# A fused cross-attention and feed-forward kernel on one core: the order of the set-up work in its opening and of a few steps between its two stages is changed

## The chip, the core and the metric

The kernel runs on one core of a Trainium2 chip. The metric is the device time of one execution in microseconds, as the median of three executions; lower is better. A core has five engines that run their own instruction streams and meet at semaphores: TensorE (PE in the profile), VectorE (DVE), ScalarE (ACT), GpSimd (POOL) and SyncE (SP), which here only issues DMAs. ScalarE issues three DMAs too.

## The reference

Sixty-four sequences of 64 tokens with 128 features each attend to a context of the same shape, then pass a feed-forward layer. The set-up draws biases and gammas that are not zero and one, so nothing can be left out.

```
def _L0_xattn_ref(x, c, Wq, bq, Wkv, bkv, q_gamma, k_gamma):
    q = x @ Wq.T + bq                       # x is the layer norm of the input
    kv = c @ Wkv.T + bkv                    # 16 heads of 8, k and v interleaved
    q = _rms_norm(q, q_gamma); k = _rms_norm(k, k_gamma)
    scores = jnp.einsum('bhnd,bhmd->bhnm', q, k) * scale
    attn = jax.nn.softmax(scores, axis=-1)
    out = jnp.einsum('bhnm,bhmd->bhnd', attn, v)
def _L0_ffn_ref(x, w1, b1, w2, b2):
    h = float2fix(jnp.einsum('bsd,df->bsf', x, w1) + b1, 8)
    h = float2fix(pwlin_gelu_basic(h, 8, 8), 8)   # linear between 33 points of an exact GELU
    return float2fix(jnp.einsum('bsf,fd->bsd', h, w2) + b2, 8)
x = x + _L0_xattn_ref(_layernorm(x), ctx_1024, ...)
x = x + _L0_ffn_ref(_layernorm(x), ...)
```

## The kernel before

The 4096 tokens are 32 tiles of 128. The attention takes two tiles a step, in 16 steps (0 to 15); the feed-forward layer takes four tiles a group, in 8 groups of two units each. Everything is written out by hand: each engine has its own program, in which `step(s)` issues that engine's share of several steps at once (a software pipeline), and every wait is on a semaphore. So each engine works strictly in the order of its code.

**A step of the attention.** GpSimd normalises x (`norm_x`, L309 to L315). TensorE transposes context and x into `bank_in` (`transpose_in`, L943 and L948), ScalarE copies that to `xcT` (L430), TensorE projects to q, q with gammas and k (`project_qk`, L955 to L964) and v (`project_v`, L974). ScalarE squares (L435), VectorE sums the squares per head (`mean_square`, L617), ScalarE takes logarithm and exponential (L441, L444), VectorE normalises (L624) and writes 16-bit high parts (L635); GpSimd writes the low parts (`lows`, L334). TensorE transposes the parts (`transpose_parts`, L992, eight matmuls for each of two tiles), ScalarE and VectorE copy them out (L450, L644), TensorE makes scores (L1006), ScalarE exponentials (L460), TensorE multiplies by v (`times_v`, L1022) and transposes back (`out_back`, L1032), and VectorE divides (`heads_out`, L664 and L666). GpSimd adds the residual (L341); VectorE takes the statistics of the second layer norm (`ln2_statistics`, L606) and applies it (`norm_x2`, L611, two instructions a step).

**Biases.** A bias enters as a matmul of a 16-bit selector (`pick16`) with `b_parts`, in which each bias row is split into three 16-bit parts. `bias_parts` makes them on VectorE in five dependent stages: cast (L719), subtract (L721), cast (L723), subtract (L725), cast (L727). This is done once for the attention's biases (384 columns) and once for those of the feed-forward layer (640 columns). Before, the bias matmul opens each accumulation (`start=True`) and the data matmuls follow.

**The opening.** SyncE loads x 0, context 0, the two gammas and `bkv` (these three broadcast to all partitions and counted by one semaphore, `small_loaded`, together with ScalarE's load of `b_q`), then x 1 to x 3 and context 1, each x waiting for the one before it, then the four loads of the feed-forward layer. VectorE clears two of the four `v_blk` buffers (L590), GpSimd the other two (L382), after its share of step -1. VectorE copies the transposed weights (L698 to L704), waits for `small_loaded`, and makes `gqk` (L732), the bias rows, `bound_sq` (L744), `wqgT` (L749) and the attention's bias parts. `bound_sq` is read by every engine (`guarded`, L226): a large value takes a branch with a slower, safe pass over all tiles; with these inputs it is not taken. No engine gets past this place before `bound_sq` is there.

**The feed-forward stage.** TensorE: `hidden` (L1128 for the bias, L1129) and `down` (L935, L1144). ScalarE rounds (L513) and evaluates the GELU at two points, `gelu_low` (L521) and `gelu_high` (L530). VectorE splits the rounded value into `f_segment` (L829) and `f_fraction` (L835), and makes `f_rise` (L842), `f_slope` (L850), `f_round` (L856) and `f_out` (L862). GpSimd adds (`f_interpolate`, L406); it waits for the slope of its own unit and the fraction of the next but one:

```
wait(pool, "slope_done", n + 1)
if gr + 1 < GROUPS:
    wait(pool, "frac_ready", n + UNITS + 1)
```

## Time and profile before

| what | value |
|---|---|
| median of three executions | 220.64 us (218.24 to 221.98) |
| profiled execution, device time | 219.01 us |
| profiled execution, span from first to last instruction | 217.1 us |
| mean granted TensorE clock | 0.959 |
| TensorE, matmuls | busy 184.1 us, 85% of the span |
| VectorE | busy 189.3 us, 87% |
| ScalarE | busy 146.3 us, 67% |
| GpSimd | busy 117.9 us, 54% |

The span starts with the first instruction, and all times in the rows count from there; 1.9 us of the profiled execution's time lie outside it. A busy share is a mean over stages with different limits, so where time can be won has to be read from the timeline. A matmul's end is modelled and overlaps the next one's start.

### The profile page before, as it was taken

Reading aid. Unit: us, or ns where it says so; the run is one execution under the profiler, and the core shown is the slowest. Engines: PE = TensorE matmul, PEld = TensorE weight load, DVE = VectorE, ACT = ScalarE, POOL = GpSimd, SP = SyncE. Lnnn points to the kernel's source line nnn. Section 1 sums busy time; section 2 is a strip of 40 time slices with the busy share of each in tenths; the row PEclk is TensorE's granted clock in tenths of the full one; section 3 lists DMA queues with packets and bytes.
Section 4 is the critical chain, followed back from the end, with each engine's and each line's share of the span. In section 5 each row is a group of like instructions: output and inputs, shape, how many; then the busy total and the mean of one; then the engine's idle time right before and its main releaser. Section 6 shows DMA issues by size and latency. Waiting matters only on the chain.

```text
span 217.1 us, 8020 instructions
## 1 busy us (share of the span) xinstructions
PE 184.1 (85%) x3308; PEld 143.5 (66%) x3308; DVE 189.3 (87%) x348; ACT 146.3 (67%) x226; POOL 117.9 (54%) x166
## 2 busy tenths in 40 slices
PE   1172889999999999999999789959799999986693
PEld 0161768888888888888888645456566566654592
DVE  6628968799999999999999757999999999999992
ACT  2021367778977778987777778867487878878511
POOL 7330864687677687767675501465165444655430
PEclk9996699999999999999999999988999999999679
DMA  4270111011211011100000000000101011010103
GB/s 110 82 206 10 51 53 49 14 44 51 54 53 49 27 32 53 51 27 29 8 3 3 3 3 2 3 0 0 48 5 48 0 48 51 0 48 0 48 0 97
DMA packets 14835, 7.95 MB, mean 37 GB/s; under 512 B 1072, under 2 KB 14576, under 8 KB 14800
## 3 DMA queue, kind: packets, MB, share of 16 engines
q1 hardware_dynamic: 14272, 7.20, 11.6%
q8 instruction: 26, 0.43, 0.8%
q10 hardware_dynamic: 528, 0.25, 0.4%
q14 instruction: 9, 0.07, 0.1%
HBM read 5.35 MB, written 2.10 MB: 34 GB/s over the span
## 4 chain that ended last, share of the span: by engine, by line
PE 44%; DVE 23%; issue 13%; POOL 13%; DMA 2%; ACT 1%; SPq 1%; DVEq 0%; POOLq 0%; ACTq 0%
POOL y_raw L406 8%; PE bank_o L1022 8%; PE banks_p L992 7%; PE banks_p L964 5%; PE banks_s L1006 5%; DVE frac L835 4%; DVE banks_p L842 4%; PE banks_p L974 4%; PE bank_o L1032 4%; PE banks_p L960 3%; DMA bkv_rep<-in_L_xattn_bkv_dram 2%; DVE y_raw L850 2%; DVE act_q L856 2%; PE banks_p L943 2%; DVE seg L829 2%
## 5 line engine op out<-in xcount | busy, mean ns | idle before, releaser
L406 POOL TENSOR_TENSOR y_raw<-g_lo,y_raw 128x1024 f32<-128x1024 f32 x15 | 35.4, 2363 | 36.4 <-DVE frac L835 35.4
L1144 PEld LDWEIGHTS bank_o<-w,act_q 128*128 128x128 f32 x224 | 29.9, 211 | 6.6 <-DVE act_q L856 5.9
L460 ACT ACTIVATE probs<-banks_s 128x512 f32<-128x512 f32 x64 | 33.0, 610 | 1.2 <-PE banks_s L1006 1.1
L334 POOL TENSOR_TENSOR parts<-qk_hat,parts 128x512 f16<-128x512 f32 x16 | 18.6, 1160 | 26.6 <-DVE parts L635 26.6
L1144 PE MATMUL bank_o<-w,act_q 128*128 128x128 f32 x224 | 31.4, 299 | 1.5 <-DVE act_q L856 1.3
L1129 PE MATMUL banks_s<-x2T,w 128*128 128x512 f32 x60 | 31.2, 602 | 0.0
L521 ACT ACTIVATE g_lo<-seg,gelu_lo 128x1024 f32<-128x1024 f32 x16 | 18.4, 1150 | 9.1 <-DVE seg L829 9.1
L530 ACT ACTIVATE banks_p<-seg,gelu_hi 128x1024 f32<-128x1024 f32 x16 | 17.9, 1118 | 8.8 <-DVE y_raw L850 8.8
L992 PE MATMUL banks_p<-ident,parts 128*128 128x128 f16 x256 | 19.6, 219 | 1.8 <-POOL parts L334 1.6
L1022 PE MATMUL bank_o<-probs,v_blk 128*32 128x64 f32 x1024 | 20.7, 222 | 0.0
L611 DVE TENSOR_SCALAR xn_all<-x_all,stats,rstd 128x128 f32<-128x128 f32 x32 | 20.1, 667 | 0.0
L850 DVE SCALAR_TENSOR_TENSOR y_raw<-banks_p,frac 128x1024 f32<-128x1024 f32 x16 | 19.6, 1224 | 0.5
L842 DVE TENSOR_TENSOR banks_p<-banks_p,g_lo 128x1024 f32<-128x1024 f32 x16 | 19.6, 1224 | 0.4 <-ACT banks_p L530 0.4
L430 ACT ACTIVATE xcT<-banks_p 128x512 f32<-128x512 f32 x16 | 9.6, 597 | 13.7 <-PE banks_p L948 13.7
L1022 PEld LDWEIGHTS bank_o<-probs,v_blk 128*32 128x32 f32 x1024 | 15.7, 109 | 3.9 <-issue 0.9
L992 PEld LDWEIGHTS banks_p<-ident,parts 128*128 128x128 f16 x256 | 14.8, 97 | 4.8 <-issue 2.0
L455 ACT ACTIVATE outT<-bank_o 128x512 f32<-128x512 f32 x16 | 9.5, 597 | 12.3 <-PE bank_o L1022 12.3
L450 ACT ACTIVATE partsT<-banks_p 128x1024 f16<-128x1024 f16 x16 | 16.4, 1022 | 0.8 <-PE banks_p L992 0.8
L513 ACT ACTIVATE hz<-banks_s,round_c 128x1024 f32<-128x1024 f32 x15 | 16.4, 1096 | 0.0
L1129 PEld LDWEIGHTS banks_s<-x2T,w 128*128 128x128 f32 x60 | 11.7, 195 | 6.8 <-issue 5.7
L943 PE MATMUL banks_p<-ident,c_in 128*128 128x128 f32 x32 | 7.4, 316 | 9.6 <-DVE wqgT L749 4.9
L654 DVE TENSOR_TENSOR v_blk<-banks_p,bv_rep 64x256 f32<-64x256 f32 x32 | 13.5, 421 | 2.1 <-PE banks_p L974 0.7
(114 smaller groups left out, 427.4 us busy)
## 6 DMA issues: line engine op xcount, KB each, us to landing
x_all<-in_x_dram SPq DMA_DIRECT2D x16, 128.0 KB, 2.9
c_in<-in_ctx_dram SPq DMA_DIRECT2D x16, 128.0 KB, 2.4
out_dram<-x_all SPq DMA_DIRECT2D x7, 256.0 KB, 2.3
w<-in_L_ffn_w_dram SPq DMA_DIRECT2D x2, 256.0 KB, 3.2
out_dram<-x_all SPq DMA_DIRECT2D x2, 128.0 KB, 1.9
b_rows<-in_L_ffn_b_dram SPq DMA_DIRECT2D x1, 192.0 KB, 3.6
wkv_raw<-in_L_xattn_Wkv_dram ACTq DMA_DIRECT2D x1, 128.0 KB, 2.9
bkv_rep<-in_L_xattn_bkv_dram SPq DMA_DIRECT2D x1, 128.0 KB, 5.4
```

What stands on the lines that cost most here:

```text
L334: g.tensor_tensor(low_slot, qk_hat[:].rearrange("p w t (h d) -> p w (t h) d", d=DH), high_slots[:, :, :, 0, :], ALU.subtract).then_inc(S[" ...
L406: g.tensor_tensor(y_raw[u][:], g_lo[n % 3][:], y_raw[u][:], ALU.add).then_inc(S[f"gelu{u}_done"], 1)
L460: a.activation(probs[i][:].rearrange("p t g n -> p (t g n)"), bank_s(i), ACT.Exp).then_inc(S["probs_ready"], 1)
L521: a.activation(g_lo[n % 3][:], seg0[u][:], ACT.Gelu, bias=gelu_lo[:], scale=1.0 / FIX).then_inc(S["glo_ready"], 1)
L530: a.activation(g_hi, seg0[u][:], ACT.Gelu, bias=gelu_hi[:], scale=1.0 / FIX).then_inc(S["ghi_ready"], 1)
L611: v.tensor_scalar(xn2_all[:, tok(s, t, 2)], x_all[:, tok(s, t, 2)], stats2[:, t, 1:2], rstd2[:, t:t + 1], ALU.subtract, ALU.mult).then_inc ...
L842: v.tensor_tensor(g_hi, g_hi, g_lo[n % 3][:], ALU.subtract).then_inc(S["rise_ready"], 1)
L850: v.scalar_tensor_tensor(y_raw[u][:], g_hi, 1.0 / SEG, frac[u][:], ALU.mult, ALU.mult).then_inc(S["slope_done"], 1)
L992: last = t_.transpose(bank_qkT[:, c0:c0 + P], rows[:, P * k:P * k + P], ident16[:])
L1022: last = t_.matmul(bank_o[ROWS * i:ROWS * i + ROWS, c0:c0 + 64], v_blk[par][:, 2 * t + b, 2 * i + gg, :, :].rearrange("p h e -> p (h e)"), ...
L1129: last = t_.matmul(out, w1[:, f0:f0 + P], x2T[gr % 2][:], start=False, stop=True)
L1144: last = t_.matmul(out, act_q[u][:, c, P * t:P * t + P], w2[:, CH // UNITS * u + c, :], start=False, stop=(u == UNITS - 1 and t == GT - 1 ...
```

## The change

It has eight parts.

1. SyncE issues the gammas and `bkv` ahead of context 0. The gammas get a semaphore of their own, `gammas_loaded`; `bkv` and `b_q` count on `bias_loaded`.
2. VectorE makes `gqk`, `bound_sq` and `wqgT` on the gammas alone, and waits for the biases only then.
3. `v_blk` 2 and 3 are cleared by ScalarE (a copy of the still empty `b_parts`) at the start, not by GpSimd after step -1. GpSimd sets the ones in all four buffers in one place (L371).
4. TensorE runs 6 matmuls of 512 columns on the 16-bit identity ahead of the weight transposes and 10 behind them, into `bank_o`, which nobody reads before it is written again.
5. In step 0 of `project_qk` the data matmuls open the accumulation, and the two bias matmuls come last and close it.
6. VectorE's share of step -1 comes ahead of the feed-forward bias work; stages 2 and 3 of that come behind its step 0, stage 4 behind its step 1.
7. `norm_x2(14)` moves ahead of `f_segment(0, 1)`; in group 1, `norm_x2(15)` moves ahead of `f_segment(2, 0)` and `f_fraction(2, 0)`.
8. TensorE's `hidden_first(0)` moves ahead of the scores of step 15.

```diff
@@ SyncE
             load_x(0)
+            for dst, src in ((gq_rep[:], gq_d.unsqueeze(0).to_broadcast([P, DH])),
+                             (gk_rep[:], gk_d.unsqueeze(0).to_broadcast([P, DH]))):
+                sp.dma_start(dst, src).then_inc(S["gammas_loaded"], 16)
+            sp.dma_start(bkv_rep[:], bkv_d.unsqueeze(0).to_broadcast([P, 2 * DIM])).then_inc(S["bias_loaded"], 16)
             load_c(0, 0)
-            for dst, src in ((gq_rep[:], gq_d.unsqueeze(0).to_broadcast([P, DH])),
-                             (gk_rep[:], gk_d.unsqueeze(0).to_broadcast([P, DH])),
-                             (bkv_rep[:], bkv_d.unsqueeze(0).to_broadcast([P, 2 * DIM]))):
-                sp.dma_start(dst, src).then_inc(S["small_loaded"], 16)
             load_x(1)
@@ GpSimd
-            pool.wait_ge(S["v_zeroed"], 2)
-            for k in range(2):
+            pool.wait_ge(S["v_zeroed"], 4)
+            for k in range(4):
...
             step(-1)
-            for k in range(2, 4):
-                g.memset(v_blk[k][:, :, :, :, :].rearrange("p b q h e -> p (b q h e)"), 0.0).then_inc(S["v_zeroed"], 1)
...
@@ ScalarE
             a.preload_act_table_set("natural_log_exp_and_others")
+            act.wait_ge(S["b_zeroed"], 1)
+            for k in range(2, 4):
+                a.activation(v_blk[k][:, :, :, :, :].rearrange("p b q h e -> p (b q h e)"), b_parts[:], ACT.Copy).then_inc(S["v_zeroed"], 1)
@@ VectorE
-            dve.wait_ge(S["small_loaded"], 16 * 4)
+            dve.wait_ge(S["gammas_loaded"], 16 * 2)
             dve.wait_ge(S["b_zeroed"], 1)
+            dve.wait_ge(S["v_zeroed"], 4)
...
+            step(-1, 3)
             scale_w1()
...
             bias_parts(ffn_bias, 1, "ffn_ready")
-            step(-1, 3)
-            for stage in range(2, 5):
-                bias_parts(ffn_bias, stage, "ffn_ready")
-            for s in range(0, LOOP_FROM):
+            step(0, 0)
+            bias_parts(ffn_bias, 2, "ffn_ready")
+            bias_parts(ffn_bias, 3, "ffn_ready")
+            step(1, 1)
+            bias_parts(ffn_bias, 4, "ffn_ready")
+            for s in range(2, LOOP_FROM):
                 step(s, s % 4)
@@ VectorE, group(gr)
+                if gr == 1:
+                    norm_x2(STEPS - 1)
                 if gr + 1 < GROUPS:
                     f_segment(gr + 1, 0)
                     f_fraction(gr + 1, 0)
-                if gr == 1:
-                    norm_x2(STEPS - 1)
@@ TensorE
+            def keep_busy(n):
+                for _ in range(n):
+                    t_.matmul(bank_o[:], ident16[:], ident16[:].unsqueeze(1).to_broadcast([P, 4, P]), start=True, stop=True)
+            pe.wait_ge(S["identity_ready"], 1)
+            pe.wait_ge(S["consts_ready"], 1)
+            keep_busy(6)
...
             last.then_inc(S["w_transposed"], 1)
+            keep_busy(10)
@@ TensorE, project_qk
+                if first:
+                    pe.wait_ge(S["w_ready"], 9)
+                else:
+                    wait(pe, "qk_normed", s)
+                    bias_qk()
...
+                if first:
+                    pe.wait_ge(S["bqk_ready"], 1)
+                    bias_qk()
+                    last = bias_q()
                 last.then_inc(S["qk_proj"], 1)
```

VectorE's order behind the weight copies was this:

```order
L732 SCALAR_TENSOR_TENSOR gqk<-gq_rep,gk_rep 128x8
L735 COPY b_rows<-b_q 96x64 x2
L738 TENSOR_TENSOR gqk_sq<-gqk 128x8
L741 COPY b_rows<-bkv_rep 96x64 x2
L744 TENSOR_REDUCE bound_sq<-gqk_sq 128x1
L746 TENSOR_TENSOR b_rows<-b_rows,gqk 96x128
L749 TENSOR_TENSOR wqgT<-wqT,gqk 128x128
L719 CAST b_parts<-b_rows 96x384
L721 TENSOR_TENSOR b_rest<-b_rows,b_parts 64x384
L723 CAST b_parts<-b_rest 64x384
L725 TENSOR_TENSOR b_rest<-b_rest,b_parts 32x384
L727 CAST b_parts<-b_rest 32x384
```

and is now this (the lines of the changed kernel are a few lower; L728 is the gamma product, L731 the maximum, L733 `wqgT`):

```order
L728 SCALAR_TENSOR_TENSOR gqk<-gq_rep,gk_rep 128x8
L730 TENSOR_TENSOR gqk_sq<-gqk 128x8
L731 TENSOR_REDUCE bound_sq<-gqk_sq 128x1
L733 TENSOR_TENSOR wqgT<-wqT,gqk 128x128
L738 COPY b_rows<-b_q 96x64 x2
L742 COPY b_rows<-bkv_rep 96x64 x2
L745 TENSOR_TENSOR b_rows<-b_rows,gqk 96x128
L714 CAST b_parts<-b_rows 96x384
L716 TENSOR_TENSOR b_rest<-b_rows,b_parts 64x384
L718 CAST b_parts<-b_rest 64x384
L720 TENSOR_TENSOR b_rest<-b_rest,b_parts 32x384
L722 CAST b_parts<-b_rest 32x384
```

The square, the maximum and `wqgT` now stand ahead of everything that reads `b_q` or `bkv`.

Behind the guard, with step -1's work beginning at the mean of squares (L617 before, L612 now), VectorE had:

```order
L790 TENSOR_SCALAR w<-w 128x512
L794 TENSOR_SCALAR b_rows<-b_rows 96x512
L719 CAST b_parts<-b_rows 96x640
L721 TENSOR_TENSOR b_rest<-b_rows,b_parts 64x640
L617 TENSOR_REDUCE ms<-qk_sq 128x64
L654 TENSOR_TENSOR v_blk<-banks_p,bv_rep 64x32x8 x2
L624 TENSOR_TENSOR qk_hat<-banks_p,rms_inv 128x512
L635 CAST parts<-qk_hat 128x2x32x16
L637 COPY parts<-minus_max 128x32
L600 BN_STATS stats<-x_all 128x6
L723 CAST b_parts<-b_rest 64x640
L725 TENSOR_TENSOR b_rest<-b_rest,b_parts 32x640
```

and now has:

```order
L612 TENSOR_REDUCE ms<-qk_sq 128x64
L649 TENSOR_TENSOR v_blk<-banks_p,bv_rep 64x32x8 x2
L619 TENSOR_TENSOR qk_hat<-banks_p,rms_inv 128x512
L630 CAST parts<-qk_hat 128x2x32x16
L632 COPY parts<-minus_max 128x32
L595 BN_STATS stats<-x_all 128x6
L786 TENSOR_SCALAR w<-w 128x512
L791 TENSOR_SCALAR b_rows<-b_rows 96x512
L714 CAST b_parts<-b_rows 96x640
L716 TENSOR_TENSOR b_rest<-b_rows,b_parts 64x640
L612 TENSOR_REDUCE ms<-qk_sq 128x64
L649 TENSOR_TENSOR v_blk<-banks_p,bv_rep 64x32x8 x2
```

The whole of step -1 moved ahead of the scaling of `w`; the next mean of squares (step 1's) follows the second stage of the bias parts directly, and the third stage comes later.

In group 1 of the feed-forward stage, from the first rise to the second, VectorE had:

```order
L842 TENSOR_TENSOR banks_p<-banks_p,g_lo 128x1024
L850 SCALAR_TENSOR_TENSOR y_raw<-banks_p,frac 128x1024
L856 TENSOR_SCALAR act_q<-y_raw 128x1024
L829 TENSOR_SCALAR seg<-hz 128x1024
L835 TENSOR_SCALAR frac<-hz 128x1024
L611 TENSOR_SCALAR xn_all<-x_all,stats,rstd 128x128 x2
L842 TENSOR_TENSOR banks_p<-banks_p,g_lo 128x1024
```

and now has:

```order
L841 TENSOR_TENSOR banks_p<-banks_p,g_lo 128x1024
L849 SCALAR_TENSOR_TENSOR y_raw<-banks_p,frac 128x1024
L855 TENSOR_SCALAR act_q<-y_raw 128x1024
L606 TENSOR_SCALAR xn_all<-x_all,stats,rstd 128x128 x2
L828 TENSOR_SCALAR seg<-hz 128x1024
L834 TENSOR_SCALAR frac<-hz 128x1024
L841 TENSOR_TENSOR banks_p<-banks_p,g_lo 128x1024
```

The two instructions of `norm_x2` (`xn_all`) now stand ahead of segment and fraction.

## Rows read from the trace of the kernel before

**Rows 1.** Busy time by stretch: stretch, us, PE, PEld, DVE, ACT, POOL, PEclk, DMA.

```profile
12.00:14.00 2.00, 2.00 (x11) 1.98 (x10) 0.43 (x1) 0.00 (x0) 1.43 (x3) 1.00 0.90 256
...
18.00:20.00 2.00, 0.00 (x0) 0.00 (x0) 1.93 (x4) 0.07 (x1) 0.00 (x0) 0.58 0.00 0
...
37.00:117.00 80.00, 79.78 (x2247) 68.00 (x2247) 75.52 (x161) 65.43 (x125) 58.63 (x98) 1.00 0.13 36
```

**Rows 2.** DMA issues: tensor, queue, size, us from issue to landing.

```profile
bkv_rep<-in_L_xattn_bkv_dram SPq DMA_DIRECT2D x1, 128.0 KB, 5.4
...
gk_rep<-in_L_xattn_k_gamma_dram SPq DMA_DIRECT2D x1, 4.0 KB, 3.7
```

**Rows 3.** Timeline of the opening, 0 to 25 us: start us, us, engine, line, operation.

```profile
1.61 0.29 POOL L353 CAST ident<-ident 128x128 f16<-128x128 f32 x1
...
2.20 1.28 ACT L424 ACT_TABLE_LOAD   x1 [2.20 <-issue]
...
2.27 0.43 SPq L259 DMA_DIRECT2D gk_rep<-in_L_xattn_k_gamma_dram  x1
...
4.36 0.63 PE L930 MATMUL banks_p<-ident,wkv_raw 128*128 128x128 f32 x2
...
8.17 0.17 DVE L732 SCALAR_TENSOR_TENSOR gqk<-gq_rep,gk_rep 128x8 f32<-128x8 f32 x1 [2.00 <-DMA bkv_rep<-in_L_xattn_bkv_dram]
...
8.59 2.56 SPq L246 DMA_DIRECT2D x_all<-in_x_dram  x2
...
8.74 0.15 DVE L744 TENSOR_REDUCE bound_sq<-gqk_sq 128x1 f32<-128x8 f32 x1
...
9.85 0.69 PE L943 MATMUL banks_p<-ident,c_in 128*128 128x128 f32 x2 [4.86 <-DVE wqgT L749]
...
11.14 0.35 DVE L727 CAST b_parts<-b_rest 32x384 f16<-32x384 f32 x1
...
11.64 0.58 PE L955 MATMUL banks_p<-b_parts,pick 128*128 128x512 f16 x1 [0.67 <-DVE b_parts L727]
...
14.36 0.63 PE L964 MATMUL banks_p<-wkT,xcT 128*128 128x128 f32 x2
...
17.04 0.43 DVE L790 TENSOR_SCALAR w<-w 128x512 f32<-128x512 f32 x1 [4.61 <-DMA b_rows<-in_L_ffn_b_dram]
...
19.21 0.69 DVE L617 TENSOR_REDUCE ms<-qk_sq 128x64 f32<-128x512 f32 x1
...
22.27 1.16 POOL L334 TENSOR_TENSOR parts<-qk_hat,parts 128x512 f16<-128x512 f32 x1 [7.57 <-DVE parts L635]
...
22.53 3.02 DVE L723 CAST b_parts<-b_rest 64x640 f16<-64x640 f32 x1
...
23.37 1.85 POOL L382 MEMSET v_blk<- 128x1024 f32 x2
```

**Rows 4.** Timeline of the opening's end, 25 to 40 us.

```profile
26.44 0.48 DVE L727 CAST b_parts<-b_rest 32x640 f16<-32x640 f32 x1
...
26.85 0.67 DVE L617 TENSOR_REDUCE ms<-qk_sq 128x64 f32<-128x512 f32 x1
...
31.26 0.39 PE L964 MATMUL banks_p<-wkT,xcT 128*128 128x128 f32 x2
...
31.97 0.61 PE L992 MATMUL banks_p<-ident,parts 128*128 128x128 f16 x8 [0.33 <-POOL parts L334]
...
38.37 0.61 PE L992 MATMUL banks_p<-ident,parts 128*128 128x128 f16 x8
```

**Rows 5.** Timeline of the hand-over and of feed-forward group 1.

```profile
131.11 1.15 ACT L521 ACTIVATE g_lo<-seg,gelu_lo 128x1024 f32<-128x1024 f32 x1 [1.32 <-DVE seg L829]
...
134.51 0.60 DVE L611 TENSOR_SCALAR xn_all<-x_all,stats,rstd 128x128 f32<-128x128 f32 x2
...
148.97 2.67 DVE L611 TENSOR_SCALAR xn_all<-x_all,stats,rstd 128x128 f32<-128x128 f32 x2
149.20 2.36 POOL L406 TENSOR_TENSOR y_raw<-g_lo,y_raw 128x1024 f32<-128x1024 f32 x1 [2.08 <-DVE frac L835]
```

53 lines of the change are left out of this document (25 added, 28 removed).

## Prediction

> **What bounds the kernel now.** I read the busy time by stretch first. Between 37 and 117 us TensorE is busy 79.78 of 80.00 us at a granted clock of 1.00, and VectorE 75.52 [rows 1]. The timeline says how long one step of that loop is: step 1's first eight transposes of `parts` start at 31.97 and step 2's at 38.37 [rows 4], so 6.40 us a step, set by TensorE. The diff touches nothing that runs in it from step 2 on. So two places are left: the opening up to 31.97, and the hand-over to the feed-forward stage with its first groups.
>
> The opening is a chain with holes. The reader should see three in the timeline [rows 3]. First, VectorE waits 2.00 us, until 8.17, for the broadcast of `bkv`; only then does it multiply the gammas, and `bound_sq` (8.74 plus 0.15) releases the branch on every engine, TensorE's first work behind it starting at 9.85. Second, projection 0 cannot start before the last cast of the biases (11.14), and TensorE ends it at 14.36 + 0.63 = 14.99. Third, VectorE waits 4.61 us, until 17.04, for the feed-forward loads, with step 0's squares already waiting; the mean of squares comes at 19.21, behind the feed-forward bias work. GpSimd's low parts of step 0 start at 22.27, after 7.57 us idle. Then GpSimd clears two blocks (23.37, 1.85 us), and VectorE's cast beside that takes 3.02 us.
>
> **The opening, part by part.** I follow the new order forwards, on the clock of the profiled run.
>
> *Warming matmuls, weights.* The 16-bit identity is there at 1.61 + 0.29 = 1.90. A 512-column 16-bit matmul at the slow level has a row of 0.58 at 11.64, the tail of which overlaps the next; I take 0.43 each, so six end at 4.5 (5.4 with the whole 0.58). The transposes of the weights, which began at about 4.1, end 0.5 later than 4.36 + 0.63 = 4.99. VectorE's weight copies, which ended 2.00 before 8.17, at 6.2, now end at 6.6. The cost of 0.5 lies in a wait (VectorE was idle to 8.17) and is hidden.
>
> *Clearing by ScalarE.* Its table load ends at 2.20 + 1.28 = 3.48. A 128x1024 activation took 1.15 us (131.11) [rows 5], so two end at 5.8, below 6.6. If each took 1.6, VectorE would wait 0.1. GpSimd's four further small memsets end long before its next statistics come.
>
> *Gammas.* `gk` landed 3.7 us after 2.27 [rows 2, 3]. It is now issued one place earlier, behind one 128 KB load fewer: 5.1 to 6.0, hidden below 6.6. Gamma product, square and maximum follow each other (0.17, 0.16, 0.15 and gaps): `bound_sq` at 7.2. TensorE follows 0.96 later (8.89 to 9.85): 8.2.
>
> *What is late next.* Two things are queued before that. Ten more warming matmuls stand from 5.4 on: at the slow level all the way they end at 9.7, at the fast one at 7.6. And the load of context 0 now stands behind `bkv`, which needed 5.4 us [rows 2]. The x tile that stood behind it before had landed when the next issue went out at 8.59 [rows 3]; I take 8.2 for the context (7.7 to 8.7). I take 8.4 for the first transposes, against 9.85.
>
> [...]
>
> *Projection 0, biases last.* Transposes and copy take some 1.3 us at the fast level: 9.7. Twelve passes at 0.11 (0.39 for a pair with its tail, at 31.26) end at 11.0. The biases are ready when `bkv` has landed (7.4 to 8.2; four instructions, 0.5 us of that chain, are done ahead): last cast at 10.8 instead of 11.5. Then two bias matmuls: projection 0 ends at 11.5 against 14.99. VectorE still does bias copies and step 1's statistics and passes the branch, so I put mean of squares 0 at 12.5, against 19.21. From there to the low parts the trace has 22.27 - 19.21 = 3.06: they start at 15.6 instead of 22.27.
>
> *The load that bounds.* `scale_w1` and the four instructions to the next mean of squares stay as they are. Their loads are issued behind x 3, whose turn depends on x 1 and x 2 landing, not on the gammas, so I leave their landing at 17.04 (16.2 to 18.0). VectorE is free at 16.1: this wait shrinks but is late next. 19.21 - 17.04 = 2.17 for the bias work: mean of squares 1 at 19.2 to 19.4, against 26.85. From there on it took before 5.12 to 31.97 [rows 4], through VectorE and GpSimd. That gives 24.4 for step 1's transposes: 7.5 us earlier. Projection 2 ends at about 23.9 if TensorE is fast, so it is hidden by 0.5.
>
> *Stages 2 to 4 of the feed-forward bias.* Before, they filled VectorE from 22.53 to 26.44 + 0.48 = 26.92, in front of step 1. The 3.02 in it is a cast that takes 0.48 with fewer rows (26.44), held by GpSimd's memsets [rows 3, 4]. Now they stand in steps 0 and 1, in which VectorE has no second statistics, no `norm_x2` (0.60 a pair if not held, at 134.51) and, in step 0, no output: more is free than the 0.36 (6.40 less 6.04) of the later steps, at least 1.0 and by my estimate up to 2. The casts can be held by `lows` (1.16) once. I cost them at nothing; without that cover, up to 2.5.
>
> **The hand-over and the groups.** `hidden_first(0)` ahead of the last scores leaves what stands ahead of `out_back` the same in sum. It is three passes of 512 columns, so the exponentials come about 1.1 us later (two at 4 x 0.11 and one 16-bit at half of that); ScalarE waited 1.32 us for `seg` at 131.11 [rows 5], so this fits with 0.2 to spare: worth nothing, -0.1 to +0.9. `norm_x2(14)` ahead of `f_segment(0, 1)` uses idle time of VectorE: 0.1. `norm_x2(15)` is the large one: its pair took 2.67 us at 148.97, and the second of it ended when GpSimd's 2.36 us addition (149.20) did; unblocked, the pair at 134.51 took 0.60 [rows 5]. Moved ahead of segment and fraction, it runs while GpSimd waits for that very fraction. The addition starts 0.6 later, but ends beside rise and slope. Gain 2.67 - 0.60 less what GpSimd then delays: 1.9 (1.3 to 2.1).
>
> [...]
>
> **Sum.** 219.01 for the profiled execution (span 217.1 and 1.9 around it) less 7.5, 1.9 and 0.1 is 209.5. The profiled execution stood 1.6 below the median of the three runs, 220.64, by which the sum would be 211.1. I take 210.4 between them.
>
> **Rivals.**
> 1. *The warming is in the way.* The clock has not risen by 8 us; the ten hold TensorE to 9.7 and projection 0 ends at about 14.9. Mean of squares 0 then comes at 15.6, VectorE reaches `scale_w1` at 19.1 with its load there, and step 1's transposes start at 26.4: 5.6 gained, not 7.5: 212.3. For it: the projection at 14.36 still ran slow though TensorE had worked since 9.85. Against: it had gaps then, and the warming starts at 1.9 and has few. 20%.
> 2. *The moved bias work is not hidden.* Casts and subtractions in steps 0 and 1 are held by GpSimd as the 3.02 was: +2.5, 212.9. Against: the memsets that held it are gone. 13%.
> 3. *The feed-forward loads land sooner*, or matter less: VectorE is free at 16.1, so 0.9 more: 209.5, and less if the branch costs less. 10%.
> 4. *The loop locks into a slower rhythm.* VectorE works 75.52 / 12.5 = 6.04 us a step of 6.40. A start with GpSimd in another phase could have it blocked once more in each step by `lows` (1.16): 7.2, +0.8 in 13 steps, 220.8, no change; by a half more of this, 7.8: +1.4 x 13 = 18, 228.6, slower. It decides from +0.75 a step. Against: the loop's order is unchanged and settled within one step before. 5%, of it slower 3%.
>
> My forecast has 52%. Time differences of under 2% are about what a measurement of this kernel can tell from none; that line is at 216.2. Cases 1 to 3 and mine lie below it: faster 0.90, the same 0.07, slower 0.03. The range: down to 207.0 for early loads and a low run, up to 214.5 for rivals 1 or 2 with a high one.
>
> **What would show it.** Right: `bound_sq` at about 7.2; TensorE's c transposes at 8.4 with passes 0.11 apart; `scale_w1` at about 17; step 1's eight transposes at 24.4; 6.40 a step; the pair of `norm_x2(15)` at 0.6. Wrong: passes 0.21 apart after 9 us, a cast near 3 us in step 0, a third wait in front of mean of squares 1, or a step above 6.5.

## The result

The changed kernel takes 210.06 us in the median of four runs (209.15 to 210.93), the kernel before 219.44 us in four runs beside it (217.44 to 221.98). The ratio is 0.960, with a 95% interval of 0.950 to 0.971: faster by 4%. (Ratios, here and below, are of means, and leave out executions more than 1.5% above the fastest of their kernel, here the one of 221.98 us.) The forecast was 210.4 us. The profiled execution took 210.93 us, the slowest of the four, with a span of 209.1 us where that of before was 217.1. TensorE's mean granted clock rose from 0.959 to 0.982; this mean says little about the opening, for which the spacing of the matmuls has to be read (see warm_tiny).

| place | before | after | forecast |
|---|---|---|---|
| `bound_sq` starts | 8.74 | 7.21 | 7.2 |
| first context transposes | 9.85 | 8.37 | 8.4 |
| projection 0 ends | 14.99 | 11.70 | 11.5 |
| mean of squares 0 | 19.21 | 12.37 | 12.5 |
| low parts 0 | 22.27 | 15.85 | 15.6 |
| mean of squares 1 | 26.85 | 19.33 | 19.2 to 19.4 |
| step 1's transposes | 31.97 | 24.47 | 24.4 |
| step 1's to step 15's transposes | 90.0 | 92.5 | 90.0 |
| step 15's transposes to the first rise | 13.05 | 11.91 | 12.95 |
| first rise to that of group 1's unit 1 | 16.54 | 14.47 | 14.6 |

First the DMA issues of the changed kernel's first 10 us (tensor, queue, size, us from issue to landing), which answer to [rows 2]:

```profile
bkv_rep<-in_L_xattn_bkv_dram SPq DMA_DIRECT2D x1, 128.0 KB, 4.5
...
gk_rep<-in_L_xattn_k_gamma_dram SPq DMA_DIRECT2D x1, 4.0 KB, 4.7
```

`bkv` lands 0.9 us sooner after its issue, `gk` 1.0 later than in [rows 2], and neither is waited for. For `gk` that is close: it lands at 1.76 + 4.7 = 6.5, where 5.1 to 6.0 was forecast, and the gamma product starts at 6.51. The timeline of the changed kernel's opening, which answers to [rows 3, 4], engine by engine (TensorE, ScalarE, VectorE, GpSimd):

```profile
2.06 2.72 PE L929 MATMUL bank_o<-ident 128*128 128x512 f16 x6 [2.06 <-POOL ident L353]
...
5.22 3.22 PE L929 MATMUL bank_o<-ident 128*128 128x512 f16 x10
8.37 0.44 PE L951 MATMUL banks_p<-ident,c_in 128*128 128x128 f32 x2
...
11.43 0.27 PE L969 MATMUL banks_p<-b_parts,pick 128*128 128x256 f16 x1
...
24.47 0.61 PE L1017 MATMUL banks_p<-ident,parts 128*128 128x128 f16 x8 [0.33 <-POOL parts L334]
31.03 0.61 PE L1017 MATMUL banks_p<-ident,parts 128*128 128x128 f16 x8
...
3.53 2.01 ACT L419 ACTIVATE v_blk<-b_parts 128x1024 f32<-128x1024 f16 x2
...
7.21 0.16 DVE L731 TENSOR_REDUCE bound_sq<-gqk_sq 128x1 f32<-128x8 f32 x1
...
12.37 0.69 DVE L612 TENSOR_REDUCE ms<-qk_sq 128x64 f32<-128x512 f32 x1 [0.93 <-ACT qk_sq L430]
...
16.71 0.57 DVE L786 TENSOR_SCALAR w<-w 128x512 f32<-128x512 f32 x1 [0.52 <-DMA b_rows<-in_L_ffn_b_dram]
...
19.33 0.69 DVE L612 TENSOR_REDUCE ms<-qk_sq 128x64 f32<-128x512 f32 x1
...
23.32 1.24 DVE L718 CAST b_parts<-b_rest 64x640 f16<-64x640 f32 x1
24.59 1.27 DVE L720 TENSOR_TENSOR b_rest<-b_rest,b_parts 32x640 f32<-32x640 f32 x1
...
15.85 1.16 POOL L334 TENSOR_TENSOR parts<-qk_hat,parts 128x512 f16<-128x512 f32 x1 [2.13 <-DVE parts L630]
```

Of the three holes one is gone and two are small: there is no wait for `bkv`, projection 0 ends 3.3 us sooner, and VectorE waits 0.93 us for its squares and then 0.52 us for the feed-forward loads, where it waited 4.61. The six warming matmuls take 0.45 each (2.72), the ten 0.32 each (3.22): TensorE turned fast among the ten, whose starts are 0.43 apart up to 6.92 and 0.22 from 7.19 on. The two context transposes behind take 0.44 together where they took 0.69.

Of the loop, the window that answers to [rows 1] (TensorE, its weight loads, VectorE, ScalarE, GpSimd, granted clock, DMA):

```profile
12.00:14.00 2.00, 0.85 (x16) 0.73 (x16) 1.28 (x3) 0.94 (x3) 1.57 (x3) 1.00 1.01 270
...
37.00:117.00 80.00, 76.10 (x2175) 64.52 (x2174) 74.13 (x157) 62.87 (x121) 55.58 (x94) 1.00 0.11 30
```

TensorE is busy 76.10 us of 80 where it was 79.78. Its timeline shows where part of that went: stretches without an issue, in the middle of the small matmuls of the scores.

```profile
41.54 0.32 PE L1031 MATMUL banks_s<-partsT 32*64 32x64 f16 x10 [0.86 <-issue]
...
81.48 0.25 PE L1031 MATMUL banks_s<-partsT 32*64 32x64 f16 x4 [0.47 <-issue]
...
100.89 0.32 PE L1031 MATMUL banks_s<-partsT 32*64 32x64 f16 x11 [0.75 <-issue]
```

`issue` means that the engine waited for nothing that the profile shows. Each such stretch lengthens its step by 0.09 to 0.16 us more than its own size (steps 3, 9 and 12 took 7.42, 6.96 and 7.29 us, where 6.40 is usual), and the steps together took 2.5 us longer than before. The kernel before has one of these too, outside the loop, in the scores of step 15:

```profile
121.97 0.61 PE L992 MATMUL banks_p<-ident,parts 128*128 128x128 f16 x8 [1.28 <-POOL parts L334]
...
125.98 0.61 PE L1006 MATMUL banks_s<-partsT 32*64 32x64 f16 x44 [0.81 <-issue]
```

The hand-over and group 1 of the changed kernel, which answer to [rows 5]:

```profile
125.19 1.15 ACT L516 ACTIVATE g_lo<-seg,gelu_lo 128x1024 f32<-128x1024 f32 x1 [0.15 <-DVE seg L828]
...
127.19 0.60 DVE L606 TENSOR_SCALAR xn_all<-x_all,stats,rstd 128x128 f32<-128x128 f32 x2 [1.09 <-POOL rstd L328]
127.70 0.69 DVE L828 TENSOR_SCALAR seg<-hz 128x1024 int32<-128x1024 int32 x1
128.31 0.69 DVE L834 TENSOR_SCALAR frac<-hz 128x1024 int32<-128x1024 int32 x1
128.91 1.23 DVE L841 TENSOR_TENSOR banks_p<-banks_p,g_lo 128x1024 f32<-128x1024 f32 x1
...
141.67 0.60 DVE L606 TENSOR_SCALAR xn_all<-x_all,stats,rstd 128x128 f32<-128x128 f32 x2
143.38 1.23 DVE L841 TENSOR_TENSOR banks_p<-banks_p,g_lo 128x1024 f32<-128x1024 f32 x1
...
143.61 2.36 POOL L398 TENSOR_TENSOR y_raw<-g_lo,y_raw 128x1024 f32<-128x1024 f32 x1 [2.59 <-DVE frac L834]
```

The pair of `norm_x2(15)` takes 0.60 where it took 2.67, since GpSimd's addition now starts after it. `norm_x2(14)` runs for the most part in a wait: the segment behind it starts 0.37 us after the end of ScalarE's rounding (127.33), where before it followed at once.

### The profile page after: what moved, and what is told of

Read it like the earlier page. It is cut to its first block, busy times and chain, and to the rows that moved or that the text cites. A ratio compares the mean times of both kernels' runs of the same rounds, so it can differ in the third digit from the quotient of the medians.

```text
span 209.1 us, 8050 instructions
## 1 busy us (share of the span) xinstructions
PE 184.6 (88%) x3324; PEld 141.1 (67%) x3324; DVE 186.9 (89%) x348; ACT 148.2 (71%) x228; POOL 117.8 (56%) x164
## 4 chain that ended last, share of the span: by engine, by line
PE 46%; DVE 22%; POOL 13%; issue 12%; DMA 3%; SPq 1%; ACT 1%; DVEq 0%; POOLq 0%
POOL y_raw L398 8%; PE bank_o L1047 8%; PE banks_p L1017 8%; PE banks_p L985 6%; PE banks_s L1031 5%; DVE frac L834 5%; DVE banks_p L841 4%; PE banks_p L999 4%; PE bank_o L1057 4%; DVE y_raw L849 3%; PE banks_p L981 3%; DVE act_q L855 2%; DMA c_in<-in_ctx_dram 2%; PE banks_p L951 2%; DVE seg L828 2%
## 5 line engine op out<-in xcount | busy, mean ns | idle before, releaser
L1169 PEld LDWEIGHTS bank_o<-w,act_q 128*128 128x128 f32 x224 | 28.8, 205 | 7.2 <-DVE act_q L855 7.0
L1169 PE MATMUL bank_o<-w,act_q 128*128 128x128 f32 x224 | 30.4, 293 | 1.8 <-DVE act_q L855 1.5
L1154 PE MATMUL banks_s<-x2T,w 128*128 128x512 f32 x60 | 30.6, 592 | 0.0
L606 DVE TENSOR_SCALAR xn_all<-x_all,stats,rstd 128x128 f32<-128x128 f32 x32 | 17.4, 584 | 1.1 <-POOL rstd L328 1.1
L1031 PE MATMUL banks_s<-partsT 32*64 32x64 f16 x1024 | 13.8, 196 | 2.5 <-issue 2.1
L1031 PEld LDWEIGHTS banks_s<-partsT 32*64 32x64 f16 x1024 | 9.9, 105 | 7.7 <-issue 5.5
```

The lines of the kernel that those rows point to most:

```text
L1031: last = t_.matmul(bank_s(i)[64 * half:64 * half + 64, c0:c0 + 64], partsT[t][rg, 1, k, cols], partsT[t][rg, 0, k, cols], start=True, stop ...
L1154: last = t_.matmul(out, w1[:, f0:f0 + P], x2T[gr % 2][:], start=False, stop=True)
L1169: last = t_.matmul(out, act_q[u][:, c, P * t:P * t + P], w2[:, CH // UNITS * u + c, :], start=False, stop=(u == UNITS - 1 and t == GT - 1 ...
```

## The experiments

Each kernel is the changed one with one edit unless said otherwise (so lines shift by a few); the ratios are to the kernel before, run beside it.

**The changed kernel once more (again).** No edit.

> The changed kernel once more, nothing edited. Theory A (the three idle stretches of TensorE of 0.5 to 0.9 us inside the scores of steps 3, 9 and 12 belong to places in its instruction stream, 256 instructions times a whole number apart): they come again at the same matmuls (after the 22nd of 32 in step 3), with sizes within 0.3 us. Theory B (they are chance of one execution): they are elsewhere or absent. By both, step 1's transposes start at 24.5 +- 0.3 and the pair of norm_x2(15) takes 0.60. Ratio to the kernel before 0.955 to 0.965.

Measured: 209.26 us, ratio 0.957 [0.950, 0.964], span 206.6 us. Step 1's transposes at 24.56, the loop 90.12, hand-over 11.91, group 1 14.48. No stretch without an issue of 0.4 us or more in the loop. So the stretches come and go with the execution, and neither theory is decided by this run (the last section comes back to their places). Against the 217.1 of before the 10.5 us of this profile are 7.41 (opening) - 0.12 (loop) + 1.14 (hand-over) + 2.06 (group 1), and the rest is rounding.

**Warming matmuls of 16 columns (warm_tiny).**

```diff
-                    t_.matmul(bank_o[:], ident16[:], ident16[:].unsqueeze(1).to_broadcast([P, 4, P]), start=True, stop=True)
+                    t_.matmul(bank_o[:, 0:16], ident16[:], ident16[:, 0:16], start=True, stop=True)
```

> The 16 warming matmuls write 16 columns instead of 512 each, so TensorE has as many instructions in the same places, but hardly any work before the first projection. [...] Theory B (the load bounds anyway): step 1 at 24.5 to 24.8, no difference in time.

Measured: 211.79 us, 0.965 [0.959, 0.971], run beside again. Step 1's transposes come at 27.66, 3.1 us later. VectorE's rows say why:

```profile
14.41 0.69 DVE L612 TENSOR_REDUCE ms<-qk_sq 128x64 f32<-128x512 f32 x1 [3.01 <-ACT qk_sq L430]
...
22.11 0.69 DVE L612 TENSOR_REDUCE ms<-qk_sq 128x64 f32<-128x512 f32 x1 [0.52 <-ACT qk_sq L430]
```

Projection 0 ran at pairs 0.43 apart and ended at 13.75, not 11.70, and projection 1 was slow as well (18.62 to 21.4), so the chain paid twice. I had put one such delay at 1.0 us, since I thought the wait for the loads would take up the rest. The granted-clock column shows none of this. It reads 1.00 through the whole opening of this run, while the pairs of the projection stand as far apart as in the opening of before (0.43):

```profile
16.00:18.00 2.00, 1.34 (x5) 0.85 (x5) 1.84 (x5) 0.21 (x1) 0.00 (x0) 1.00 0.03 8
```

In the changed kernel the same pairs stood 0.22 apart (10.1 to 11.1), under the same 1.00. So in these traces the column does not tell the two levels apart before its first change, and this run has the highest mean of all, 0.991, with the slowest opening of those that keep part 6.

**Twice as many warming matmuls of half the width (warm_split).**

```diff
-                for _ in range(n):
-                    t_.matmul(bank_o[:], ident16[:], ident16[:].unsqueeze(1).to_broadcast([P, 4, P]), start=True, stop=True)
+                for i in range(2 * n):
+                    half = bank_o[:, 256 * (i % 2):256 * (i % 2) + 256]
+                    t_.matmul(half, ident16[:], ident16[:].unsqueeze(1).to_broadcast([P, 2, P]), start=True, stop=True)
```

> Each warming matmul of 512 columns is cut into two of 256: the same work and time, but 32 more instructions on TensorE (16 matmuls with their weight loads). Theory A (idle stretches belong to places in the instruction stream): the stretch of step 3 moves 16 matmuls towards the start, from after the 22nd to after about the 6th of the 32 scores, the others likewise by 16 matmuls; their sum may change by up to 2 us either way. Theory B (a wait for data or a semaphore): they stay after the 22nd, or vanish for no reason. Opening the same by both, step 1 at 24.5 +- 0.3.

Measured: 209.14 us, 0.956 [0.949, 0.963], span 206.7. The same columns warm as well (passes of projection 0 0.11 apart, as in again); the work in front is as in again (mean of squares 1 at 19.51). Step 1's transposes came at 25.19, because TensorE, which had little to do around 20 us, ran projection 2 slow (granted 0.82 in 20 to 22 us, 0.50 in 22 to 24). No stretch of 0.4 us without an issue in its loop, so nothing could move, and the theories stay open here too.

**The kernel before with norm_x2(15) moved (only_norm15).**

```diff
+                if gr == 1:
+                    norm_x2(STEPS - 1)
                 if gr + 1 < GROUPS:
                     f_segment(gr + 1, 0)
                     f_fraction(gr + 1, 0)
-                if gr == 1:
-                    norm_x2(STEPS - 1)
```

> The kernel before, with norm_x2(15) alone moved ahead of segment and fraction of group 2. Theory A (the pair was held by GpSimd's addition): the pair takes 0.60 instead of 2.67, and the second rise of group 1 follows the first addition of group 1 1.9 to 2.1 us sooner than before; time 1.9 us less, ratio 0.991. Theory B (the hold only moves to the next VectorE instruction): the pair 0.6, but the next rise or slope takes longer, time less by under 0.5 us.

Measured: 216.65 us, 0.987 [0.981, 0.993], beside again. The pair takes 0.60, and from the first rise to the one behind it 14.49 us against 16.54:

```profile
148.18 0.60 DVE L611 TENSOR_SCALAR xn_all<-x_all,stats,rstd 128x128 f32<-128x128 f32 x2
149.90 1.22 DVE L842 TENSOR_TENSOR banks_p<-banks_p,g_lo 128x1024 f32<-128x1024 f32 x1
```

This part alone is worth 2.05 us at that place. Its scores of step 15 stop for 1.03 us, with 44 matmuls left, as in before (0.81).

**The feed-forward bias work back ahead of step -1 (ffn_bias_back).** Part 6 undone.

```diff
-            step(-1, 3)
             scale_w1()
...
-            step(0, 0)
-            bias_parts(ffn_bias, 2, "ffn_ready")
-            bias_parts(ffn_bias, 3, "ffn_ready")
-            step(1, 1)
-            bias_parts(ffn_bias, 4, "ffn_ready")
-            for s in range(2, LOOP_FROM):
+            step(-1, 3)
+            for stage in range(2, 5):
+                bias_parts(ffn_bias, stage, "ffn_ready")
+            for s in range(0, LOOP_FROM):
```

> The changed kernel with part 6 undone: VectorE again does the scaling and two stages of the feed-forward bias ahead of its step -1, and stages 2 to 4 behind it. Theory A (this part carries most of the opening's gain, since VectorE otherwise waits for the loads at 16.7 with step 0's squares there at 12.3): mean of squares 0 at 18.9 instead of 12.4; the cast of stage 2 is now at most 1.3 us long (held by lows, no memsets beside it) instead of 3.02; step 1's transposes at 28.5 to 29.5 against 24.5; time 4 to 5 us more than the changed kernel (about 213.8). Theory B (the rest of the opening gives the gain): less than 2 us more.

Measured: 214.85 us, 0.980 [0.973, 0.986]. Step 1's transposes come at 32.01, as in before (31.97). Earlier gammas, biases and clears save nothing here: VectorE waits 5.84 us for the loads, and in the meantime TensorE stands idle and its clock falls (to 0.50, below).

```profile
17.27 0.43 DVE L786 TENSOR_SCALAR w<-w 128x512 f32<-128x512 f32 x1 [5.84 <-DMA b_rows<-in_L_ffn_b_dram]
...
26.41 0.69 DVE L612 TENSOR_REDUCE ms<-qk_sq 128x64 f32<-128x512 f32 x1 [0.58 <-ACT qk_sq L430]
```

And its busy time by stretch, columns as in [rows 1]:

```profile
18.00:20.00 2.00, 0.00 (x0) 0.00 (x0) 1.90 (x4) 0.00 (x0) 0.00 (x0) 0.50 0.00 0
...
22.00:24.00 2.00, 1.74 (x8) 1.22 (x7) 2.00 (x4) 0.60 (x1) 1.49 (x2) 0.50 0.22 66
24.00:26.00 2.00, 2.00 (x14) 1.94 (x13) 1.76 (x3) 0.22 (x1) 1.88 (x3) 0.50 0.22 66
```

I had expected that the cast without GpSimd's memsets would still gain 2.5 us or more (28.5 to 29.5). The cast did shrink, from 3.02 to 1.24 us, but projection 1, at a granted clock of 0.50 until 25.7, set the next mean of squares (it waited 0.58 us for the squares), so that came 0.44 sooner than before; and the transposes and copies of `parts` behind that slow projection were no sooner than before (VectorE's copy at 28.37, before 28.33). Two limits had stood side by side, and only one was lifted.

**GpSimd clears again (gpsimd_clears).** Part 3 undone: two memsets and their ones behind GpSimd's step -1, none on ScalarE.

```diff
             step(-1)
+            for k in range(2, 4):
+                g.memset(v_blk[k][:, :, :, :, :].rearrange("p b q h e -> p (b q h e)"), 0.0).then_inc(S["v_zeroed"], 1)
...
-            for k in range(2, 4):
-                a.activation(v_blk[k][:, :, :, :, :].rearrange("p b q h e -> p (b q h e)"), b_parts[:], ACT.Copy).then_inc(S["v_zeroed"], 1)
```

> The changed kernel with part 3 undone: GpSimd clears the two buffers and sets their ones behind its step -1. Theory A (the memsets hold VectorE's cast and delay norm_x(2)): they start at about 17.0 and end, with the ones, at 19.9; a feed-forward bias cast of VectorE beside them takes 1.5 us or more instead of 0.79; norm_x(2) ends at 22.6 instead of 19.8, step 1's transposes at 25.9 to 26.5; 1.5 to 2 us more. Theory B (hidden, because step 1 waits for VectorE's bias work and not for GpSimd): step 1 at 24.5 to 25.0.

Measured: 210.74 us, 0.963 [0.957, 0.970]. Step 1's transposes at 25.95, 1.4 to 1.5 later. GpSimd's and VectorE's rows:

```profile
16.91 1.85 POOL L382 MEMSET v_blk<- 128x1024 f32 x2
```

```profile
17.92 1.11 DVE L790 TENSOR_SCALAR w<-w 128x512 f32<-128x512 f32 x1 [1.76 <-DMA b_rows<-in_L_ffn_b_dram]
...
20.81 0.69 DVE L617 TENSOR_REDUCE ms<-qk_sq 128x64 f32<-128x512 f32 x1
```

The memsets hold the scaling of `w`: it takes 1.11 instead of 0.43 when free [rows 3], and ends 0.27 us after them (18.76). But it also starts 1.21 us later than in the changed kernel, because the load itself is later: it was issued at 12.54, not at 11.94, and lands 5.4 us after its issue, not 4.8. The issue times vary between executions with the same order (11.44 to 11.94), so this run mixes a late load with the memsets. By an estimate from these rows the memsets make 0.7 us of the delay of the scaling and the load 1.1 (a shorter cast behind gives 0.3 back); what the clears cost alone is not shown.

**Biases first in step 0 (bias_first).** Part 5 undone: `first = False` in `project_qk`, with the waits for the weights put ahead of it.

> The changed kernel with part 5 undone: projection 0 starts with its bias matmuls and so waits for the last cast at about 10.5. Theory A (VectorE's wait of 0.52 us in front of the scaling hides up to that much): projection 0 ends 0.6 to 0.7 later, mean of squares 0 at about 13.0, VectorE reaches the scaling with its load there, step 1's transposes at 24.5 to 24.8, time within 0.4 us of the changed kernel. Theory B (all passes through): step 1 at 25.2.

Measured: 210.02 us, 0.959 [0.953, 0.966]. Mean of squares 0 at 13.31 (0.8 later than in again), mean of squares 1 at 20.10 (0.8 later), step 1's transposes at 25.41: theory B.

**The small loads behind context 0 again (loads_back).** Parts 1 and 2 half undone: SyncE's old order, and VectorE waits for all of them, but keeps its own new order.

```diff
+            load_c(0, 0)
             for dst, src in ((gq_rep[:], gq_d.unsqueeze(0).to_broadcast([P, DH])),
...
-            load_c(0, 0)
...
             dve.wait_ge(S["gammas_loaded"], 16 * 2)
+            dve.wait_ge(S["bias_loaded"], 16 * 2)
```

> The changed kernel with parts 1 and 2 half undone: context 0 is loaded ahead of gammas and bkv again, and VectorE waits for bkv before it touches the gammas (its own order stays new). Theory A: gamma product at about 8.1, bound_sq at 8.8, first transposes at 9.7 instead of 8.4 and still at the fast clock, mean of squares 0 at about 13.5, step 1's transposes at 25.0 to 25.6, 0.5 to 1.1 us more. Theory B (hidden by the feed-forward loads): step 1 at 24.5 to 24.8.

Measured: 211.15 us, 0.966 [0.957, 0.974]. `bound_sq` at 7.98, mean of squares 0 at 13.12, mean of squares 1 at 20.04, step 1's transposes at 25.37. Its VectorE row and GpSimd row:

```profile
16.81 1.17 DVE L787 TENSOR_SCALAR w<-w 128x512 f32<-128x512 f32 x1
```

```profile
16.55 1.15 POOL L334 TENSOR_TENSOR parts<-qk_hat,parts 128x512 f16<-128x512 f32 x1 [2.06 <-DVE parts L630]
```

In both runs the scaling no longer waits for a load. It takes 1.17 us, where 0.43 is its time when free [rows 3], and ends 0.28 us after GpSimd's `lows(0)` (17.70), which itself follows the mean of squares 0. A delay of 0.6 to 0.8 us there arrives at step 1 whole. The 0.52 us wait for the load in the changed kernel is no cover. Again shows the same limit with no wait for a load at all:

```profile
16.11 1.17 DVE L786 TENSOR_SCALAR w<-w 128x512 f32<-128x512 f32 x1
...
15.85 1.16 POOL L334 TENSOR_TENSOR parts<-qk_hat,parts 128x512 f16<-128x512 f32 x1 [1.95 <-DVE parts L630]
```

Its scaling is free to start 0.6 us sooner than the changed kernel's, and ends at the same 17.28.

**The scores of step 15 first again (hidden_back).** Part 8 undone.

```diff
+            scores(last_step, 0)
+            scores(last_step, 1)
             pe.wait_ge(S["ffn_ready"], 2)
             pe.wait_ge(S["qk_normed"], STEPS)
             pe.wait_ge(S["x2_t_copied"], 2)
             hidden_first(0)
-            scores(last_step, 0)
-            scores(last_step, 1)
```

> From step 15's transposes to the first rise took 13.05 us in the kernel before (13.26 with the move of norm_x2(15) alone) and 11.91 with the whole change. Of the 1.14, 0.81 is a stretch in the scores of step 15 in which TensorE issues nothing, and 0.33 is left for the order. A (the stretch hangs on the place in TensorE's instruction stream, moved by what was added in the opening; the order is worth 0.33): with the scores ahead of the first hidden matmuls again, no such stretch in the scores of step 15, 12.2 us, whole time +0.3. B (the order does it all, for the stretch comes from ScalarE and VectorE reaching their work in another phase): the stretch of 0.8 to 1.0 is back, 13.0 to 13.3, whole time +1.1. C (my forecast: order worth nothing): 11.9.

Measured: 210.17 us, 0.962 [0.956, 0.968]. From step 15's transposes (115.56) to the first rise (127.48) 11.92 us: C. ScalarE ends its exponentials sooner and waits longer for the same segment:

```profile
123.76 1.15 ACT L516 ACTIVATE g_lo<-seg,gelu_lo 128x1024 f32<-128x1024 f32 x1 [1.34 <-DVE seg L828]
```

**Parts 7b and 8 on the kernel before (norm15_hidden).** The last two edits together on the kernel before (part 8 in its forward direction).

> The kernel before with norm_x2(15) and with hidden_first(0) ahead of the scores of step 15; its opening is that of before. A (the stretch without an issue hangs on the place in the instruction stream): it is still there, now with 47 instead of 44 of the 64 matmuls of the scores left since three matmuls moved ahead of them, 0.8 to 1.0 us long, and from the transposes to the first rise 12.7 to 12.9 us instead of 13.26. B (the order takes the stretch away): 11.9 us, and the whole 1.3 us below only_norm15.

Measured: 216.55 us, 0.989 [0.986, 0.992]. No stretch without an issue in the scores of step 15, and 12.09 us to the first rise, between A and B and neither. The whole time shows no gain over only_norm15 (0.989 against 0.987), where B had 1.3 us. A stretch of 0.51 us showed in step 14 instead, with 13 matmuls left. Everything ahead of step 14 is the same stream as in only_norm15, so the stream alone does not fix where TensorE stops. Its feed-forward loads let VectorE go at 15.91, not at 17.04, and step 1's transposes came at 30.86 where before had 31.97: in the old order the landing of these loads goes straight into the time.

**Feed-forward bias work spread over more steps (spread).**

```diff
             step(-1, 3)
+            step(0, 0)
             scale_w1()
...
             bias_parts(ffn_bias, 0, "ffn_ready")
+            step(1, 1)
             bias_parts(ffn_bias, 1, "ffn_ready")
-            step(0, 0)
+            step(2, 2)
             bias_parts(ffn_bias, 2, "ffn_ready")
+            step(3, 3)
             bias_parts(ffn_bias, 3, "ffn_ready")
-            step(1, 1)
-            bias_parts(ffn_bias, 4, "ffn_ready")
-            for s in range(2, LOOP_FROM):
-                step(s, s % 4)
...
             ln2_statistics(STEPS - 3)
+            bias_parts(ffn_bias, 4, "ffn_ready")
```

> A (VectorE's chain sets step 1, and steps 1 to 4 have room for a stage each): in the changed kernel 1.4 to 1.5 us of feed-forward bias work (scaling 0.5 to 1.2, the row scaling and stages 0 and 1) stand between step 0's and step 1's mean of squares. With them behind step 0, the mean of squares of step 1 comes at 17.9 instead of 19.3 and step 1's transposes at 23.3 to 23.6 instead of 24.5, unless projection 2 bounds them (it ended at about 24). The loop stays at 6.40 a step from step 4 on, the whole is 0.5 to 1.1 us below the changed kernel. B (VectorE's steps have too little room once the loop has begun, 6.04 of 6.40 us): stages of up to 1.2 us in steps 1 to 3 hold those steps up by as much, steps of 6.8 to 7.4 us there, and the last cast sits in the hand-over: same time as the changed kernel or up to 1.5 us more.

Measured: 209.22 us, 0.958 [0.952, 0.963], span 207.1: no gain over again. Step 1's transposes at 24.62. The wait only changed its name: mean of squares 1 stands at 19.24 with 2.99 us of waiting for the squares, since TensorE's clock fell between projections 0 and 1 (busy time by stretch):

```profile
14.00:16.00 2.00, 1.35 (x5) 0.66 (x5) 1.86 (x5) 0.60 (x1) 0.10 (x1) 0.65 0.87 262
16.00:18.00 2.00, 1.99 (x10) 1.99 (x11) 0.25 (x1) 0.00 (x0) 2.00 (x4) 0.50 0.19 50
```

In again the clock had fallen in the same way (0.62 and 0.53 in these two stretches); there the squares ended at 19.15, 0.2 us before VectorE came for them, a third limit at the same place. Steps 3 and 4 took 6.75 and 7.08 us, so B holds for stages 2 and 3 in the loop; the last cast in the hand-over cost nothing (11.90).

**Spread, with TensorE kept busy through steps 0 and 1 (spread_busy).** The edit is shown against spread.

```diff
             def transpose_in(s, par):
+                if isinstance(s, int) and s in (1, 2):
+                    keep_busy(4)
...
                     last = bias_q()
                 last.then_inc(S["qk_proj"], 1)
+                if first:
+                    keep_busy(2)
...
             bias_parts(ffn_bias, 1, "ffn_ready")
+            bias_parts(ffn_bias, 2, "ffn_ready")
             step(2, 2)
-            bias_parts(ffn_bias, 2, "ffn_ready")
             step(3, 3)
-            bias_parts(ffn_bias, 3, "ffn_ready")
...
             ln2_statistics(STEPS - 3)
+            bias_parts(ffn_bias, 3, "ffn_ready")
             bias_parts(ffn_bias, 4, "ffn_ready")
```

> spread again, with two edits. TensorE multiplies into the unread bank in its idle stretches of steps 0 and 1 (2 matmuls of 512 columns behind projection 0, 4 ahead of each of the context transposes 1 and 2), and VectorE's stages sit where spread showed room (scaling and stage 0 behind step 0, stages 1 and 2 behind step 1, stages 3 and 4 in the hand-over). In spread TensorE's granted clock was 0.65 and 0.50 in 14 to 18 us, so that step 1's mean of squares waited 2.99 us for ScalarE's squares until 19.24. A (that slow projection 1 took the gain of the spreading): the clock stays at 1.00 from 12 to 24 us, projection 1 ends at 17.3, mean of squares 1 comes at 17.9, step 1's transposes at 23.1 to 23.5, and the time is 1.0 us below that of the repeated changed kernel: about 208. B (GpSimd's and VectorE's shares of step 0 bound the opening, whatever TensorE does): step 1's transposes at 24.4 to 24.7, time 209. C (the matmuls come in the way of the work behind them): 25 or later.

Measured: 207.94 us in five runs (207.12 to 208.40), 0.952 [0.948, 0.955], span 205.3, the fastest kernel of the study. Its busy time in the same stretches, then the mean of squares 1 and step 1's transposes:

```profile
14.00:16.00 2.00, 1.66 (x11) 1.05 (x11) 1.87 (x5) 0.60 (x1) 0.35 (x1) 1.00 0.73 205
16.00:18.00 2.00, 1.68 (x22) 1.52 (x23) 0.24 (x2) 0.86 (x2) 2.00 (x4) 1.00 0.20 59
```

```profile
17.77 0.69 DVE L612 TENSOR_REDUCE ms<-qk_sq 128x64 f32<-128x512 f32 x1 [1.76 <-ACT qk_sq L430]
...
23.20 0.61 PE L1021 MATMUL banks_p<-ident,parts 128*128 128x128 f16 x8
```

A, number by number. Ten more matmuls of no use (2, 4 and 4) and the same bias work in other places bring step 1 forward by 1.4 us against again, and the span by 1.3. The two edits were not tried apart, and this is the one trace with both. The intervals of the ratios of again and spread_busy overlap (0.950 to 0.964, 0.948 to 0.955), so the size of this gain rests on the traces.

## Why the prediction was right, and where it was not

**The opening: right, 7.5 forecast and 7.50 measured, in again 7.41.** Every station of the chain in the table came within 0.25 us. The sum has TensorE fast from the first context transposes on, and no row of before shows that warming brings this about. The runs show it: behind the warming the passes of projection 0 stood 0.11 apart, in warm_tiny 0.21, which put step 1's transposes 3.1 us later and the median 2.5 higher. `hidden_first(0)` and the clears by ScalarE (1.0 us each, over at 5.54) came out as costed, the stages 2 to 4 within 0.2 us.

**The step on what bounds it failed.** "The load that bounds" said that VectorE waits for the feed-forward loads until 17.04 and that this wait is late next. In the profiled execution the row indeed names the load, for 0.52 us. But bias_first and loads_back show that 0.6 to 0.8 us of delay ahead of it pass through whole, with no load in the row: GpSimd's `lows(0)` holds the scaling for 1.17 us, whether it starts at 16.11 (again) or at 16.89. In the changed kernel the load lets VectorE go at 16.71 and `lows(0)` ends at 17.01, and I had seen only one of them. The number was right because both lie at the same place, and that is luck. By the same step I took the sum to be the same whether the warming makes TensorE fast or not, since that load comes later: warm_tiny says 3.1 us. It also made me put warm_tiny at 1.0 us and bias_first at no more than 0.4. By spread and spread_busy the next limit behind these two is the clock of projection 1 (0.65 and 0.50 in 14 to 18 us in spread, 1.00 in spread_busy), and behind that the projection itself, with mean of squares 1 at 17.77.

**The opening's gain is not a sum over its parts.** With part 6 undone it is nothing (32.01 against 31.97), and with one of the others undone most of it stays: 6.6 without the load order, 6.6 without the late biases, 6.0 without the clears (in a run with a late load), 4.3 without the warming. Part 6 removes the load from the chain; the others shorten what then is the chain.

**Stages 2 to 4 in steps 0 and 1 cost 0.17 us, though they are held for more.** The cast took 1.24 (free: 0.47 at 38.21 in spread), behind `lows(1)` at 23.05, and the subtraction behind it 1.27 (free: 0.79 at 44.96 in spread), beside GpSimd's normalisation. Step 1 took 6.56 us in the changed kernel and 6.57 in again, against 6.40 before, since mean of squares 2 now follows the subtraction directly; from step 1 to step 15 again took 90.12 us against 90.0. Beside GpSimd the subtraction took 0.48 us more than its 0.79, of which at most 0.17 is in the time. Rival 2 falls, because VectorE had the room.

**The hand-over: the mechanism right, 0.1 forecast and 1.14 measured.** `hidden_first(0)` is worth nothing, as said: hidden_back has 11.92 us where the changed kernel has 11.91, and ScalarE's wait for the segment takes up the difference (0.15 against 1.34 us). The rest has two parts. 0.81 is the stretch without an issue in before, which the later kernels did not have there. It stands in both traces with that opening and that order (before, only_norm15) and in none of the twelve others, so it counts as won, but by accident: nothing in the prediction aimed at it. Some 0.2 is `norm_x2(14)`: from the end of ScalarE's rounding to the first rise before took 1.76 us (133.26 to 135.02), hidden_back 1.57 (125.91 to 127.48), and norm15_hidden, with part 8 but without this move, is 0.18 slower than the changed kernel. For the last 0.15 two causes are left: such a stretch cost 0.09 to 0.16 beyond its own size in the loop too, or part 8 is worth it where `norm_x2(14)` has not moved (only_norm15 less its stretch 12.23, norm15_hidden 12.09).

**Group 1: 1.9 forecast, 2.07 measured.** I had taken off 0.2 for the later start of GpSimd's addition; nothing of it arrived.

**The loop: right in the mean, wrong in the profiled execution.** Rival 4 did not come about: from step 2 on most steps of again take 6.40 us, none more than 6.57. The 2.5 us that the profiled execution lost there are stretches without an issue, absent in again. They may make a good part of the spread between runs of one kernel (209.15 to 210.93), but only the profiled executions have a trace.

**The total.** Forecast were 9.5 us off the profiled execution. In again 10.5 came off the span (1.0 more in the hand-over, 0.2 more in group 1), in the profiled changed kernel 8.0, since the stretches in the loop took 2.5. The medians differ by 9.4, the means behind the ratio by 8.7. So the nearness of 210.06 to 210.4 is in part luck: more was won than forecast in the hand-over and in group 1, stretches took some of it back, and the 0.9 us that I added to the sum of 209.5 for a higher median had no ground, since the kernel before had medians of 218.6 to 219.3 in the later sets of runs.

## What to carry to other kernels

When a wait in front of an instruction is removed, look at its duration as well as at its wait: here GpSimd's `lows(0)` held the scaling of `w` and ended at 17.01 in the changed kernel, 0.30 us behind the load, and where no load was waited for (again) this second limit showed only as a long row with no bracket, 1.17 us instead of 0.43. In this opening with holes, TensorE's clock was one of the limits that ran beside the chain: with the engine kept busy through the holes of steps 0 and 1, not only ahead of the first matmul, the granted clock in 14 to 18 us was 1.00 instead of 0.65 and 0.50, and step 1's transposes came at 23.20 instead of 24.62 (spread_busy against spread, which differ in the places of two bias stages too). So keep it busy there before judging what the other engines' order is worth. And undo the parts one at a time: here one part, undone, took the whole gain of the opening with it, and the others were worth 0.8 to 3.1 us each at step 1's transposes only beside it.
